# Attention's ten weight chunks laid 4192 bytes apart instead of 4096

## What is computed

```python
x = x + attn(cond(x, cond_128, ...), in_proj_w, conv_weight, ...)
x = x + ffn(cond2(x, cond_128, ...), qweight, lut4, lut8, bias)
# inside attn, for h = hidden_states (128*32 tokens x 512):
proj = einsum('bld,pd->blp', hidden_states, in_proj_w)   # gate, x, B, C, dt
conv = conv_bias + sum_k pad[:, k:k+L] * conv_weight[:, k]; xBC = silu(conv)
state = state * dA_t + dtx_t * B_t;  y_t = einsum(state, C_t)
yn = groupnorm(y + x*D) * norm_weight * silu(gate)
out = einsum('bli,di->bld', yn, out_proj_w)
```

## The kernel before

| matmul | weights | streamed | streamed minus weights, modulo 512 |
|---|---|---|---|
| projections, L837 | wt: 163808 + 4096 n + 512 (4 l + k), always 480 | ht: 204768 + 8192 rr + 2048 k, always 480 | 0 |
| output projection, L932 | gy: 122432 + multiples of 512, always 64 | wot: 68992 + multiples of 2048, always 384 | 320 |
| segment sum, L874 | mask_gtr: 29088, so 416 | segr: 139200 + multiples of 2048, so 448 | 32 |
| feed-forward, L1341 | x3t: 94816 + multiples of 512, so 96 | wq: 28064 + multiples of 2048, so 416 | 320 |

## Time and profile before

### The profile page before, as it was taken

One profiled execution on the slowest core, in us unless ns is written; L12 is line 12 of the kernel. 1 busy time (PEld: TensorE's weight loads), 2 busy tenths in 40 slices (PEclk: granted clock), 3 DMA queues, 4 the chain that ended last, 5 costly groups with the idle time before them and its releaser, 6 DMA issues. The chain is left out here.

```text
span 3563.1 us, 58721 instructions
## 1 busy us (share of the span) xinstructions
PE 3478.4 (98%) x19789; PEld 2874.5 (81%) x19789; DVE 3082.2 (87%) x4843; ACT 1459.6 (41%) x2218; POOL 477.3 (13%) x334
## 2 busy tenths in 40 slices
PE   6699999999999999999999999999999999999999
PEld 4488888888888888888888888888888888888888
DVE  6589999999999999999999999999999999998443
ACT  3444444444444444444444444444444444444111
POOL 3201111011111011111011111011111011110333
PEclk9799999999999999999999999999999999999999
DMA  7722335332533353333533363334433363335331
GB/s 235 264 101 105 119 142 184 116 129 106 200 130 116 114 189 130 118 129 117 195 129 108 116 212 118 111 129 162 145 129 118 112 212 109 115 129 161 100 93 57
DMA packets 220673, 490.29 MB, mean 138 GB/s; under 512 B 39595, under 2 KB 85067, under 8 KB 211043
## 3 DMA queue, kind: packets, MB, share of 16 engines
q1 hardware_dynamic: 216964, 488.88, 39.3%
q0 software_dynamic: 304, 0.82, 0.1%
q10 hardware_dynamic: 3376, 0.26, 0.1%
HBM read 320.51 MB, written 169.39 MB: 137 GB/s over the span
## 5 line engine op out<-in xcount | busy, mean ns | idle before, releaser
L837 PE MATMUL p_cv<-ht,wt 128*128 128x512 f32 x5376 | 1298.6, 394 | 4.4 <-DMA ht<-h_d 4.4
L837 PEld LDWEIGHTS p_cv<-ht,wt 128*128 128x128 f32 x5376 | 1000.7, 188 | 230.2 <-issue 15.6
L932 PE MATMUL bank<-wot,gy 128*128 128x512 f32 x3072 | 737.4, 396 | 0.0
L932 PEld LDWEIGHTS bank<-wot,gy 128*128 128x128 f32 x3072 | 567.3, 188 | 128.1 <-issue 11.0
L982 ACT ACTIVATE xc<-p_cv,cvb,cvw 128x512 f32<-128x512 f32 x256 | 199.8, 780 | 933.4 <-PE p_cv L837 933.4
L1067 DVE SCALAR_TENSOR_TENSOR xc<-p_cv,cvw,xc 128x496 f32<-128x496 f32 (+2 forms) x768 | 545.2, 717 | 31.4 <-ACT xc L982 7.9
L837 PE MATMUL bank<-ht,wt 128*128 128x512 f32 x2304 | 562.0, 393 | 0.0
L837 PEld LDWEIGHTS bank<-ht,wt 128*128 128x128 f32 x2304 | 427.8, 188 | 87.9
L811 POOL TENSOR_TENSOR r<-rv,neg_half 128x4 f32<-128x4 f32 x64 | 90.0, 1407 | 2453.3 <-DVE rv L1155 2453.3
L1089 DVE TENSOR_TENSOR m<-cbm,y 128x1024 f32<-128x1024 f32 x256 | 301.6, 1220 | 7.8
L1067 DVE SCALAR_TENSOR_TENSOR xc<-bank,cvw,xc 128x496 f32<-128x496 f32 (+2 forms) x384 | 275.6, 718 | 33.4 <-ACT xc L982 21.7
(11 more groups left out here) (187 smaller groups left out, 3632.9 us busy)
## 6 DMA issues: line engine op xcount, KB each, us to landing
ht<-h_d SPq DMA_DIRECT2D x64, 2048.0 KB, 7.8
acc<-acc_d SPq DMA_DIRECT2D x64, 1024.0 KB, 7.4
wt_d<-wnext SPq DMA_DIRECT2D x128, 512.0 KB, 3.4
acc_d<-acc SPq DMA_DIRECT2D x64, 1024.0 KB, 4.3
wt<-wt_d SPq DMA_DIRECT2D x70, 512.0 KB, 8.4
stage<-in_L_attn_in_proj_w SPq DMA_DIRECT2D x106, 256.0 KB, 2.7
h_d<-ht_out SPq DMA_DIRECT2D x8, 2048.0 KB, 7.9
wot<-wt_d SPq DMA_DIRECT2D x28, 512.0 KB, 6.0
```

Source lines behind the costliest of these rows:

```text
L837: ins = pe.matmul(pb[:, :], wt[:, n, l, k, :], ht[:, rr, k, :], start=(q == 0 and k == 0), stop=(q == 2 and k == KC - 1))
L932: ins = pe.matmul(bank[OUT[t]][:, :], gy[:, c, l, t * P:(t + 1) * P], wot[:, rr, c, :], start=(c == 0 and q == 0), stop=(c == CT - 1 and q ...
```

## The change

The ten chunks of `wt` become rows of 1048 elements, of which the first 1024 are used, so that they lie 4192 bytes apart. `TOP` goes down by 960 bytes to make room, so `ht` (204768) and `acc` stay exactly where they were. `wt` starts at 162848, which is 32 modulo 512. Streamed minus weights modulo 512 is then 448, 352, 256, 160, 64, 480, 384, 288, 192 and 96 for chunks 0 to 9. Within a chunk the slices still lie 512 bytes apart, so all 12 matmuls of a chunk have the same distance. Stage 3's tensors that are counted from `TOP` all start 960 bytes lower. No instruction is added, removed or moved on any engine.

```diff
-TOP = 163808
-WT_BYTES = 4 * NPJ_ALL * 2 * DM
+WT_ROW = 2 * DM + 24
+TOP = 162848
+WT_BYTES = 4 * NPJ_ALL * WT_ROW
...
-        wt, ht, acc = sh.wt, sh.ht, sh.acc
+        wt = sh.wt[:, :, 0:2 * DM].rearrange("p n (a k c) -> p n a k c", a=2, k=KC)
+        ht, acc = sh.ht, sh.acc
...
-        sh.wt = at_top("wt", [P, NCV + CT, 2, KC, P], 0, F32R)
+        sh.wt = at_top("wt", [P, NPJ_ALL, WT_ROW], 0, F32R)
```

## The result

| | before | changed |
|---|---|---|
| median | 3559.89 us (4 runs, 3559.45 to 3560.44) | 3587.88 us (4 runs, 3586.57 to 3591.77) |
| ratio | | 1.0080, 95% interval 1.0064 to 1.0096 |
| span of the profiled execution | 3563.1 us | 3584.8 us |

The change costs 28.0 us, 0.79%, more than the 12 us of the forecast and inside its range. The first place to look is stage 2's length on PE, because stage 1 did not end at the same moment in the two profiled executions. The view of single lines, before and after, gives the first and last start of a group.

The account below looks back on a forecast made before the run. PE's matmul pace in stage 2 was taken as the bound. Chunks 0 to 5 +12.2 us, chunks 6 to 9 and everything else 0, on the median 3560.1, gave 3572 us; range 3541 to 3590, the forecast's own 3565 to 3581.

Parts of the forecast that it names:

- the forecast: Stage 2 projections: the settled rhythm is lost in chunks 0 to 5, +7 to +16 us; chance 0.46.
- its own signs: PE timeline: chunks 0 to 5 take 16.5 to 16.6 us, chunks 2 to 4 run at 229 to 231 ns.
- What bounds the kernel: Stage 2's time is the number of PE's matmuls times their pace; PE's waits come to only 17.2 us.
- The term of chunks 0 to 5: Stage 2's 72-matmul stretch: each chunk's new distance makes a new start, +0.19 us an iteration, +12.2 us over 64.
- The upper bound of +0.25: Chunks 0 to 5 all at chunk 6's unsettled 230.8 ns: 16.62 us in place of 16.37.
- Chunks 6 to 9: Single chunks of stage 2, unsettled every time: taken as 0, bounds -0.20 and +0.08 us an iteration.
- Everything else: Stage 3's convolution reads, the reloads and the copies filling the first chunks: taken as 0, with 1.2 us of doubt.
- Slower and more: Rival: projections run at the segment sum's 232.5 ns everywhere, +0.45 us an iteration, +29 us, 3589 us; chance 0.08.
- No effect: Rival: the projections' pace differs by rhythm and entry, not by address; time 3560 us; chance 0.26.
- the rule of the two independent ports: PE's streamed operand and weight loads have separate read ports, so no distance matters and the time stays 3560 us.
- Less collision, faster: Rival: distance 0 makes weight load and streaming collide, others are better; -16 us (0.12) or -67 us (0.08); chance 0.20.

Follow-up runs that it names:

- the run by distance: Separate kernel without the computation, 60 matmuls at each distance between streamed and weight tiles: 226.8 ns at 256, 229.2 at 64, 233.2 at 32 and 192.

## Why the prediction was right, and where it was wrong

That the time lies inside the stated range is owed to a rival that had 0.08: the forecast's own range ended at 3581 (its lower end is given once as 3567, once as 3565), and its own signs failed. It wanted 16.5 to 16.6 us for chunks 0 to 5, which took 16.72, and at most 231 ns for chunks 3 and 4, which ran at 232.

**What bounds the kernel** held. Stage 2 is PE's pace: +26.3 us between its first and last matmul, with PE's waits at 17.7 us against 17.2 and DMA share and clock as before.

**The term of chunks 0 to 5** was mis-sized, and its reason was wrong. Predicted +0.19 us, bounded by +0.11 and +0.25; measured +0.35, 22.4 us of the whole. The step that failed is the prediction's sentence that "a rhythm can last for at most 12 matmuls, and twelve are about what it takes to settle today". Constant 192 gave +0.40 us with nothing to settle anew, and 0 and 64 in turn gave +0.08 us, with a change at each chunk. A rhythm found anew is seen in chunk 2 alone, 0.04 of the 0.35 us. What acts in the rest is the value of each distance: 233 to 234 ns for most, 229 for 64 and 226.7 for 0. The upper bound of +0.25 came from chunk 6's unsettled run, though a row with a higher pace stood beside it: the segment sum at distance 32, 232.5 to 233 ns, which the run by distance showed to be that distance's lasting pace. I had used it in a rival only.

**Chunks 6 to 9** were taken as 0. They cost 0.04 us an iteration, 2.6 us in all, within the bounds given; leaving them at distance 0 made stage 2 2.8 us shorter.

**Everything else** at 0 held: the move by 960 bytes, which carries stage 3's tensors with it, cost nothing in the run where it was done alone.

**The rivals.** *Slower and more*, at 0.08, named the pace (232.5) and the time (3589) that came. It was the right mechanism; I gave it too little, since I thought of the new distances as unknown around the known three, while two of the three known were slow. Distance 32, which the prediction calls long-lived, stood on four matmuls only; the run by distance bore it out. *No effect* fell, and with it the rule of the two independent ports (the Trainium skill, page "SBUF — State Buffer", section "Who interferes with whom") as the prediction read it, that no distance matters: the distance alone, in a kernel with nothing else in it, moves the pace from 226.8 to 233.2 ns. *Less collision, faster* fell with its sign: distance 0 is the best one, not the worst. The 216 ns of the Trainium skill, page "TensorE: Matmul & The Clock Gate", section "Back-to-back issue gap", are met by bfloat16 (215.8) and by no float32r distance. That section gives the 216 for isolated matmuls and about 131 ns for a sustained stream of this width; no run here comes near the 131, and the measurement decides.

**What stays open.** Why a distance has its pace. Runs with fewer weight columns show that distances 0 and 192 no longer differ at 32 columns, and that the pace is then 18.6 ns over 213.3, more than the 13.4 of 128 columns at 0. Alternating residues didn't tell a matmul's own weights from those loaded meanwhile. Why a chunk sometimes has to find its rhythm anew (chunk 2 of the changed kernel, chunk 7 before the move by 960 bytes) is open as well. A conflict of the two reads for a part of the memory fits the dependence on distance, and that bfloat16 has none between 0 and 192, but it was not shown.

## What to carry to other kernels

With float32r operands on a saturated TensorE, look at the byte distance between streamed operand and weights in a partition, modulo 256: tensors whose sizes and starts are multiples of 256 have the distance 0 by themselves, and padding that breaks this cost 0.8% here. Smaller tensors in between break it as well: the output projection of the kernel before stands at 320, which is 64 modulo 256, at 228.9 ns. From 228.9 to 226.7 over its 3072 matmuls would be an estimated 7 us, which no run here tried. When a change replaces one value by many unknown ones, take the price from where most of the other rows lie, not from the nearest to the present value. And test a layout idea with a small kernel first: one run of 330 us, 1200 matmuls, gave the whole table.

## What was not expected of the hardware

- Float32r matmuls of 128x512 at the granted clock of 1.00 have a pace that depends on the distance modulo 256 of their operands: 226.8 ns at 256, 229.0 to 229.2 at 64 and 320, 228.3 at 16, 233.2 at most others, 234.4 at 160, and 230.7 to 232.4 at 48, 248 and 252.
- bfloat16 in the same kind of loop: 215.8 ns at 0, and a row as long at 192.
- Fewer weight columns do not make such a matmul steadily faster: at distance 0 it takes 226.8 ns with 128, 230.2 with 96 and 231.9 with 32; at 192 it takes 233.2, 228.5 and 231.9.
- Two distances in turn from one matmul to the next, 0 beside 64 and 192, ran at 231.4 to 231.6 ns in either order, so neither the distance to a matmul's own weights nor that to the weights loaded meanwhile sets its pace alone.
- The entry of a run depends on more than its own distance: wt and ht both 960 bytes lower made chunk 7 0.05 us shorter, at the same distance 0, and distance 0 (mod 256) took 2.72 us for twelve matmuls behind a chunk at 64 but 2.76 behind one at 96 (mod 256).
